# One-hots and filter products of two units in one VectorE instruction each: the edge stage of a graph layer

## The reference, cut to what matters

```python
xn = layernorm(h) * ln_w + ln_b
w_phys = (silu(rbf @ w1 + b1) @ w2 + b2) * cutoff[:, None]
msg_phys = xn[col] * w_phys
q_e, k_e, v_e = Q[row], K[col], V[col]          # 8 heads of 32
scores = sum(q_e * k_e, -1) / sqrt(32) * cutoff
attn = softmax(scores, axis=1)                  # over the 8 heads of one edge
combined = msg_phys + gate * attn * v_e
aggr = segment_sum(combined, row)
out = h + aggr @ wo + bo
```

## Time and profile before

| | us |
|---|---|
| median of 3 runs | 6098.5 |
| lowest, highest | 6062.72, 6134.49 |
| span of the profiled execution | 6313.9 |
| profiled span less the median | 215.4 |
| of the span: up to the first unit of the edge stage | about 3066 |

### The profile page before, as it was taken

The page is one execution under the profiler, slowest core; times in us unless marked ns, Lnnn a source line. Parts: engine busy times, 40 slices in busy tenths (PEclk is TensorE's granted clock), DMA queues, the critical chain, the costliest instruction groups (busy, mean ns, idle before and its releaser), DMA issues. The chain is left out here.

```text
span 6313.9 us, 119829 instructions
## 1 busy us (share of the span) xinstructions
PE 5449.7 (86%) x25068; PEld 4056.7 (64%) x25069; DVE 4650.8 (74%) x11811; ACT 3223.8 (51%) x12137; POOL 3930.5 (62%) x3579
## 2 busy tenths in 40 slices
PE   3788989889888888898689898989888889988889
PEld 3455656566655556565467777777777777777777
DVE  8788856555544444322599999999999999999995
ACT  4223222232222223222477777777777777777774
POOL 1566756666665655555566666666666666666661
PEclk9889999999999999999899999999999999999999
DMA  8334334334433433333699998888988889889835
GB/s 279 105 106 143 109 131 144 107 128 145 140 104 133 139 102 129 130 117 110 242 330 303 303 303 302 300 301 300 307 297 298 295 299 304 302 303 304 304 107 171
DMA packets 488183, 1337.77 MB, mean 212 GB/s; under 512 B 90385, under 2 KB 167993, under 8 KB 485629
## 3 DMA queue, kind: packets, MB, share of 16 engines
q0 software_dynamic: 230240, 887.66, 41.2%
q1 hardware_dynamic: 206920, 371.04, 18.1%
q10 hardware_dynamic: 50850, 77.03, 3.4%
HBM read 1074.68 MB, written 350.21 MB: 226 GB/s over the span
## 5 line engine op out<-in xcount | busy, mean ns | idle before, releaser
L956 POOL DMA_INDIRECT ukvx<-kvx_table,udst x1856 | 2104.2, 1134 | 1034.6 <-issue 470.2
L328 POOL DMA_INDIRECT records<-rows,slot_i x1660 | 1752.0, 1055 | 1117.8 <-DVE rows L581 521.5
L661 PE MATMUL w_ps<-w2s,hid 128*128 128x256 f32 x6656 | 1628.8, 399 | 209.5 <-DVE rows L581 186.7
L661 PEld LDWEIGHTS w_ps<-w2s,hid 128*128 128x128 f32 x6656 | 1285.7, 199 | 578.3 <-DVE rows L581 228.6
L767 ACT ACTIVATE hid<-hid_ps,b1t 128x512 f32<-128x512 f32 x832 | 526.5, 683 | 1890.9 <-PE hid_ps L650 921.6
L581 DVE TENSOR_TENSOR rows<-w_ps,b2b 128x512 f32<-128x512 f32 x832 | 568.6, 685 | 1165.0 <-PE w_ps L661 535.4
L1055 PE MATMUL uq_ps<-aggr,uonehotT 128*128 (+1 forms) x3712 | 1037.4, 402 | 315.8 <-issue 160.3
L1073 PE MATMUL ag_ps<-ukvx,uonehot 128*128 128x256 f32 x3712 | 954.9, 380 | 26.4 <-ACT uonehot L990 26.4
L1069 PE MATMUL ag_ps<-ukvx,uonehot_cut 128*128 128x256 f32 x3712 | 956.2, 380 | 0.0
L1055 PEld LDWEIGHTS uq_ps<-aggr,uonehotT 128*128 128x128 f32 x3712 | 633.6, 190 | 464.9 <-issue 411.8
L1073 PEld LDWEIGHTS ag_ps<-ukvx,uonehot 128*128 128x128 f32 x3712 | 705.5, 190 | 125.3 <-issue 28.3
(11 more groups left out here) (171 smaller groups left out, 5213.5 us busy)
## 6 DMA issues: line engine op xcount, KB each, us to landing
urec<-records SPq DMA_DIRECT2D x928, 260.0 KB
rbf_in<-in_edge_attr SPq DMA_DIRECT2D x207, 256.0 KB
kvx_table<-kvx ACTq DMA_DIRECT2D x10, 3456.0 KB
ukvx<-kvx_table,udst POOLq DMA_INDIRECT x1856
records<-rows,slot_i POOLq DMA_INDIRECT x1661
records<-kvx SPq DMA_DIRECT2D x1, 25480.0 KB
fbase<-x_plus_h SPq DMA_DIRECT2D x14, 896.0 KB, 7.1
out<-fout SPq DMA_DIRECT2D x13, 896.0 KB, 4.9
```

The costliest lines, as they stand in the source:

```text
L328: pool.indirect_dma_start(recs, bass.IndirectOffsetOnAxis(ap=slot_i[:, q, t:t + 1], axis=0), rows[:, q, t, :], None).then_inc(scattered[q] ...
L661: m = pe.matmul(w_ps[j % 2][:, h, :], hid[:, k % 2, c, h, j * P:(j + 1) * P], w2s[:, c, :], start=(h == 0 and c == 0), stop=(c == 1), skip ...
L956: pool.indirect_dma_start(kvx[:, k, j, :], None, table, bass.IndirectOffsetOnAxis(ap=dst_i[:, k, j:j + 1], axis=0), bounds_check=NPAD - 1, ...
```

## The change

`select` now works on a pair: in even units VectorE makes the one-hots of units u+4 and u+5 in one `tensor_tensor` comparison of 4 times 128 elements, whose two inputs are the bf16 row of numbers (repeated four times) and the four float32 places of the records (each repeated 128 times). It waits for the records of both units, and for `cut_ready`, `share_ready` and `turned` of one unit more than before. In odd units VectorE makes the filter products of units u-1 and u in one `tensor_tensor` of 4 times 256 elements. Both raise their semaphore by 2. Even units thus have no `physical`, odd units no `select`. The argument `begin` of `aggregate` that nothing used goes away.

```diff
             def select(u, k, i, first):
                 dve.wait_ge(rec_in[k], i * 16 + 16)
+                dve.wait_ge(rec_in[k + 1], i * 16 + 16)
                 if not first:
-                    dve.wait_ge(s["cut_ready"], u - (DEPTH - 1))
-                    dve.wait_ge(s["share_ready"], u - (DEPTH - 1))
-                    dve.wait_ge(s["turned"], u - (DEPTH - 1))
-                for j in range(2):
-                    m = dve.tensor_scalar(ohb[:, k, j, :], iota_bf[:], rec[:, k, j, R_LOC:R_LOC + 1], None, ALU.is_equal)
-                m.then_inc(s["onehot_ready"], 1)
+                    dve.wait_ge(s["cut_ready"], u - (DEPTH - 2))
+                    dve.wait_ge(s["share_ready"], u - (DEPTH - 2))
+                    dve.wait_ge(s["turned"], u - (DEPTH - 2))
+                dve.tensor_tensor(ohb[:, k:k + 2].rearrange("p k j e -> p (k j) e"), iota_bf[:].unsqueeze(1).to_broadcast([P, 4, P]),
+                                  rec[:, k:k + 2].rearrange("p k j f -> p (k j) f")[:, :, R_LOC:R_LOC + 1].to_broadcast([P, 4, P]), ALU.is_equal).then_inc(s["onehot_ready"], 2)
...
             def physical(u, k, i, first):
-                dve.tensor_tensor(kvx[:, k, :, 2 * H:3 * H], rec[:, k, :, 0:H], kvx[:, k, :, 2 * H:3 * H], ALU.mult).then_inc(s["phys_done"], 1)
+                both = kvx[:, k - 1:k + 1].rearrange("p k j f -> p (k j) f")[:, :, 2 * H:3 * H]
+                dve.tensor_tensor(both, rec[:, k - 1:k + 1].rearrange("p k j f -> p (k j) f")[:, :, 0:H], both, ALU.mult).then_inc(s["phys_done"], 2)
...
-            for k in range(SELECT_AHEAD):
+            for k in range(0, SELECT_AHEAD, 2):
                 select(k, k, 0, True)
...
             def unit(u, k, i, first, last):
                 query_key(u, k, i, first)
-                physical(u, k, i, first)
-                ahead(select, SELECT_AHEAD, u, k, i, first, last)
+                if k % 2:
+                    physical(u, k, i, first)
+                else:
+                    ahead(select, SELECT_AHEAD, u, k, i, first, last)
                 score(u, k, i, first)
```

More of the change, by code:

```diff
@@ L1056, in query, with aggregate @@
                 m.then_inc(s["qe_done"], 1)
-            def aggregate(u, k, former, b, begin):
+            def aggregate(u, k, former, b):
                 if isinstance(u, int) and u == 0:
@@ L1092, in unit @@
                 if not (first and k < LAG):
-                    aggregate(u - LAG, (k - LAG) % DEPTH, None if first and k == LAG else near[k], near[k + 1], first)
+                    aggregate(u - LAG, (k - LAG) % DEPTH, None if first and k == LAG else near[k], near[k + 1])
             def asked(i, k):
@@ L1105, in _ @@
             for n in range(LAG):
-                aggregate(UNITS - LAG + n, DEPTH - LAG + n, rest[n], rest[n + 1], False)
+                aggregate(UNITS - LAG + n, DEPTH - LAG + n, rest[n], rest[n + 1])
         @block.vector
```

## The result

The changed kernel takes 6134.03 us (median of 18 runs, 6101.09 to 6156.73), the kernel before 6077.09 (18 runs, 6050.84 to 6134.49). The ratio is 1.0085, with a 95% interval of 1.0065 to 1.0105: slower by 0.65 to 1.05%, within 1% by the median, but on the other side than the forecast and above its range.

The account below looks back on a forecast made before the run. VectorE was taken to bound the edge stage at 3.14 us a unit. Comparison 0.06 and product 0.07 us a pair, taken as 0.12, over 464 pairs save 56 us: 6098.5 to 6042.5 us, range 5995 to 6112 (own range 6015 to 6070).

Parts of the forecast that it names:

- The instructions: VectorE in the edge stage: merged comparison 0.60 us, product 1.13, gapless pair of units 6.15 instead of 6.28.
- rival two: VectorE's merged comparison runs fast with bf16 beside float32, saving 0.27 us more a pair: 5917 us; chance 0.06.
- What bounds the stage: Edge stage: VectorE's 3.14 us a unit sets the pace over TensorE's 2.87; profiled waits before L1125 mostly absent when timed.
- the sum: Edge stage: 0.12 us saved a pair over 464 pairs, 56 us, VectorE's mean unit going from 3.14 to 3.08.
- Rival one: Edge stage: TensorE's semaphores set the pace at 3.35 us, VectorE only waits more, time stays 6098; chance 0.25.
- Waits: `select`'s waits for one unit more cost nothing, as ScalarE and TensorE finished that unit over two microseconds before.
- Records: SyncE's load of even units' records starts 2.5 us later, costing nothing while the landing takes under 6.8 us.
- rival three: Records reach ScalarE's destinations of even units too late, costing 139 us less the 56: 6182 us; chance 0.07.
- rival four: The comparison's two SBUF inputs hold off GpSimd's gathers, 0.30 us a unit, some saving lost: 6042 to 6100; chance 0.10.

Follow-up runs that it names:

- the first series: Follow-up runs on a level without late TensorE semaphores; the kernel before, unchanged, took 5663.07 us.
- the third series: Follow-up runs on the result's own level; the kernel before took 6098.11 us, the changed kernel 6134.51, the changed kernel with `select` behind `score` 6148.99.
- less product: Kernel before with the filter product made for 227 of 256 features: 5609.09 us (0.9906) without lag, 6312.54 us (1.0002) with strong lag.
- the products alone: Kernel before with only the filter products in pairs, one-hots unit by unit: 1.0019 without lag, 0.9984 with strong lag.
- the one-hots alone: Kernel before with only the one-hots in pairs, products unit by unit: 0.9977 without lag, 1.0013 on the result's level.
- The padded kernel: Changed kernel with one small extra VectorE reciprocal behind `select` in even units: 6244.63 us, 0.9901 of the kernel before.

## Why the prediction was wrong

- *The instructions* (comparison 0.60, product 1.13, pair 6.15): right, to the hundredth. As rival two had it otherwise, it fell. In the mean the saving is 0.057 a unit. The cost of a merged instruction can be read off its row, but neighbours can change with it: with the product alone in pairs they took all of it back.
- *What bounds the stage*: this step failed. "Such a wait is not TensorE's workload" was right: the same matmuls leave 1.1 us of waits before L1125 in the first series. "In timed runs they are mostly absent, and VectorE's 3.14 us sets the stage" was concluded from the 215.4 us between profile and median, which I took for the profiler's doing. It was a difference between executions. For the kernel before the conclusion was still nearly true, by luck: on the level of the result its waits before L1125 are 27.9 us by the page of the third series, not 178.2. What failed is what the sum made of it, that VectorE goes on setting the pace when it is 0.06 us a unit faster, with no term for waits for TensorE's late query. The waits went from 0.032 to 0.126 us a unit, some 87 us in the stage against the 56 forecast as saved. The other levels show how the worth of VectorE's time changes: with no lag its 3.13 does set the stage (less product: -0.94%); with strong lag 0.06 us a unit less, and 0.03 more, change nothing.
- *Rival one* was the nearest: "TensorE's semaphores, not VectorE's queue, pace the stage", with VectorE waiting 0.06 more. It waits 0.094 more than before of its own level, so the time doesn't stay but rises. That TensorE's late results could take back more than the saving was in no rival.
- *Waits*, "I put it at nothing": `select` waits 21.3 us in 749 units, where it had waited for nothing. The argument counted two microseconds of ScalarE's lead from its load alone; with the lag ScalarE gets its inputs late too (between 3400 and 5800 us of the kernel after L977 waits 134.4 us for TensorE's transposes). It is a third of the new waits, but moving it away gave nothing back (the third series).
- *Records*, rival three: 0.21% by itself on the level with strong lag. Its 6.8 us are about right (6.75 in the median from the issue to the first reader, even units of the kernel after) and enough in the running stage: the landing of 7.1 us that it went by was another load's, and in the first series these loads land in 2.6 to 6.5 us, 5.1 in the median. They are too little in the first hundred units, beside the query table's loads. (By the earlier trace rows L1140 ends 2.41 us into the unit, not 2.45; nothing hangs on it.)
- *GpSimd*, rival four: a gather takes 1214 ns on average after and 1225 before in the third series; no hold-off shows in that.

What the runs settle: the change saves VectorE's time, and on the level of the result more than that comes back as waits, two thirds of them before L1125, which needs TensorE's query. Why there are more of these waits stays open. That the unit of 2.81 us outruns TensorE's 2.87 and the one of 3.34 then can't catch up is argued and not shown, and the products alone speak against it: their units are more uneven, and with strong lag they add no waits. On the level of the result they weren't run. That TensorE gets its one-hots two at a time is argued too; the one-hots alone wait 0.092 there against 0.032, but with a time that can't be told from before's.

Open too is why the same change gains 0.7 to 0.9% with strong lag. The padded kernel and the one with less product speak against VectorE's load as the reason, and the products alone give -0.16% with an interval that takes in no change. The one-hots alone weren't run there, nor the changed kernel without lag. No version was shown better than the kernel before on all levels: the one-hots alone are 0.23% faster without lag and not with some, the change with smaller query loads 1.0% faster with strong lag.

## What to carry to other kernels

Before an excess of a profile over the timed runs is put down to the profiler, look for a timed run's own span; if it lies beside its time, the profile is of a slower execution, and its waits belong to that execution. Count the semaphore updates in the trace before a silence between them is read. Where a second engine needs 2.87 us for what the bounding one does in 3.14, a saving of 0.06 is worth something only if the second one's results come on time: ask for each kernel what a wait costs if they come late. Merging the instructions of two steps saves fixed costs, and also moves their neighbours and tightens waits. Lay the whole repeating pattern, start to start, beside the old one: here the paired product saved 0.07 us and its neighbours took 0.07.

## What the runs showed of the hardware

- The same kernel runs at 5661, 6077 to 6113 or 6295 to 6310 us, with durations of VectorE's instructions equal to a few ns and a granted clock of 0.99 to 1.00 in the edge stage after its first 100 units on each. What differs there is how long TensorE's semaphores come behind its recorded matmuls: 0.39 us without exception, or 1.5 to 1.8 in the median and 2.6 to 2.8 for the slowest tenth of the queries whose update is recorded. What sets the level wasn't found. The Trainium skill ("Perfetto Trace Analysis", § Tensor Engine Instruction (MATMUL, LD_WEIGHTS)) says that a matmul's end in a profile is computed from its size and not observed. The traces agree, and show how far the two can part: the row alone wouldn't tell the 0.39 from the 2.8.
- A trace can hold fewer than half of the semaphore updates: about 100,000 at the level of 5661 us, 39,500 to 43,200 at the others, for all engines' semaphores.
- VectorE's instructions lengthen by 25 to 50 ns at fixed places of a repeating pattern (L1158, 0.65 instead of 0.60 us to the next start in nearly every even unit of the kernel with paired products; the first of four comparisons in a row, four taking 0.70 us where two times two took 0.66), with no wait shown before them.
- A comparison that has bf16 on one side and float32 on the other takes 682 ns for 512 elements, as two float32 inputs do (684). The Trainium skill ("VectorE: DVE Perf Modes", § The perf-mode tier table) has `tensor_tensor` in its single-rate mode for float32 and at twice that rate for bf16, and no row for a mixed pair; here the mixed pair took the time of float32.
